# A two-layer graph network with residual and normalisation: the main loop with three row groups in flight on a ring of four PSUM pairs

## The reference

```python
def _sage_conv(x, src, dst, W_l, b_l, W_r):
    agg = jax.ops.segment_sum(x[src], dst, num_segments=N_NODES)
    deg = jax.ops.segment_sum(jnp.ones((src.shape[0],), x.dtype), dst, num_segments=N_NODES)
    return (agg / jnp.maximum(deg, 1.0)[:, None]) @ W_l + b_l + x @ W_r
h = jax.nn.relu(_sage_conv(x, src, dst, W1_l, b1, W1_r))
h = jax.nn.relu(_sage_conv(h, src, dst, W2_l, b2, W2_r))
out = _layernorm(x + h @ W3 + b3, axis=-1)
```

## Time and profile before

| what | value |
| --- | --- |
| median of 3 runs (lowest, highest) | 3318.33 us (3307.94 to 3328.46) |
| span of the profiled execution | 3317.4 us |
| TensorE matmul busy | 2928.3 us (88%) |
| VectorE busy | 2695.7 us (81%) |
| ScalarE busy | 1899.9 us (57%) |
| GpSimd busy | 2689.2 us (81%) |

### The profile page before, as it was taken

One profiled execution on the slowest core, in us unless ns is written; L12 is line 12 of the kernel. 1 busy time (PEld: TensorE's weight loads), 2 busy tenths in 40 slices (PEclk: granted clock), 3 DMA queues, 4 the chain that ended last, 5 costly groups with the idle time before them and its releaser, 6 DMA issues. The chain is left out here.

```text
span 3317.4 us, 57863 instructions
## 1 busy us (share of the span) xinstructions
PE 2928.3 (88%) x18433; PEld 2638.2 (80%) x18433; DVE 2695.7 (81%) x5026; ACT 1899.9 (57%) x3188; POOL 2689.2 (81%) x2614
## 2 busy tenths in 40 slices
PE   6999898999998998999989999999989698787876
PEld 5888887888887888888878888888878687676775
DVE  5778788877888788888988988888888787777775
ACT  4656555556665555655555656556555465555654
POOL 5888888888888888888888888888888767777776
PEclk9999999999999999999999999999999898898988
DMA  3444434434443434434344343444434455555553
GB/s 114 140 145 133 151 128 139 139 127 148 137 139 133 144 130 144 139 127 158 133 142 143 132 157 125 142 142 143 139 127 158 164 199 188 166 201 186 175 191 120
DMA packets 253118, 488.23 MB, mean 147 GB/s; under 512 B 37615, under 2 KB 165206, under 8 KB 253090
## 3 DMA queue, kind: packets, MB, share of 16 engines
q1 hardware_dynamic: 202498, 387.58, 34.2%
q0 software_dynamic: 50176, 99.91, 9.9%
q10 hardware_dynamic: 416, 0.40, 0.0%
HBM read 284.67 MB, written 206.22 MB: 148 GB/s over the span
## 5 line engine op out<-in xcount | busy, mean ns | idle before, releaser
L908 PE MATMUL ps_y<-w_hi,h_hi 128*128 128x256 f32 x1960 | 584.3, 298 | 180.4 <-DVE h_lo L683 180.1
L683 DVE TENSOR_TENSOR h_lo<-h_full,h_hi 128x512 fp32r<-128x512 f32 x784 | 712.3, 946 | 34.3 <-ACT h_hi L511 24.8
L384 POOL TENSOR_SCALAR o<-y,rs,nb 128x256 f32<-128x256 f32 x784 | 659.7, 850 | 1.7 <-DMA out_dram<-o 1.7
L509 ACT ACTIVATE h_full<-ps_h,bias 128x512 f32<-128x512 f32 x784 | 538.3, 687 | 197.1 <-PE ps_h L897 169.5
L908 PE MATMUL ps_y<-w_lo,h_hi 128*128 128x256 f32 x1960 | 572.5, 292 | 0.0
L908 PE MATMUL ps_y<-w_hi,h_lo 128*128 128x256 f32 x1960 | 572.5, 292 | 0.0
L342 POOL DMA_INDIRECT xe<-in_x_dram,e_stage x392 | 412.7, 1053 | 177.2 <-issue 94.8
L908 PEld LDWEIGHTS ps_y<-w_hi,h_hi 128*128 128x128 f32 x1960 | 396.6, 202 | 200.0 <-issue 189.1
L503 ACT CAST xt_hi<-ps_x 128x512 fp32r<-128x512 f32 x392 | 210.9, 590 | 596.1 <-PE ps_x L887 596.1
L669 DVE TENSOR_TENSOR xt_lo<-ps_x,xt_hi 128x512 fp32r<-128x512 f32 x392 | 252.7, 686 | 334.2 <-ACT xt_hi L503 334.0
L396 POOL TENSOR_TENSOR xb<-xn,b_row 128x1024 f32<-128x1024 f32 x196 | 477.1, 2434 | 35.7 <-DVE nb L719 32.2
(11 more groups left out here) (121 smaller groups left out, 7054.1 us busy)
## 6 DMA issues: line engine op xcount, KB each, us to landing
xn<-in_x_dram SPq DMA_DIRECT2D x196, 512.0 KB, 6.6
out_dram<-o SPq DMA_DIRECT2D x196, 512.0 KB
seg<-seg_tab SPq DMA_DIRECT2D x74, 512.0 KB, 4.6
xdb_tab<-xdb SPq DMA_DIRECT2D x49, 512.0 KB, 3.9
h_tab<-src_h SPq DMA_DIRECT2D x49, 512.0 KB
h_tab<-dst_h SPq DMA_DIRECT2D x49, 512.0 KB
xn<-h_tab SPq DMA_DIRECT2D x49, 512.0 KB, 5.2
xb<-xdb_tab SPq DMA_DIRECT2D x49, 512.0 KB, 4.1
```

Of the source, the lines that this page charges most:

```text
L384: ins = nc.gpsimd.tensor_scalar(o[:, b, s], y[:, b, s], rs[:, b, s:s + 1], nb[:, b, s:s + 1], ALU.mult, ALU.add)
L509: nc.scalar.activation(h_full[:, n, k], ps_h[n][:, k], ACT.Relu, bias=bias[:, n, k:k + 1]).then_inc(hf_ok[n], 1)
L683: nc.vector.tensor_tensor(h_lo[:, n, k], h_full[:, n, k], h_hi[:, n, k].bitcast(f32), ALU.subtract).then_inc(hlo_ok[n], 1)
L908: ins = nc.tensor.matmul(ps[:, s // 2, s % 2 * D:(s % 2 + 1) * D], a[:, k, s * P:(s + 1) * P], wx[:, w, k], start=first, stop=end)
```

## The change

Outside the functions printed, the change renames the PSUM pairs, drops `xe_full` and adapts counts. What it does:

- The four pairs become a ring, `pair[0]` to `pair[3]`. At step g (u = g mod 4), `pair[u]` holds the transposes of g+2 and later the second layer of g, `pair[u+1]` the first layer of g+1, `pair[u+2]` the edge quarter, `pair[u+3]` the third layer of g-1.
- TensorE's step becomes: transposes (g+2), first layer (g+1), edge quarter, third layer (g-1), second layer (g).
- Low parts, high parts, the residual and the edge sums `src_h`, `dst_h` are one instruction of 1024 columns each. The relu stays at 512, since its bias differs by half.
- The edge rows are read from PSUM directly, by the cast to `xe_hi`, the subtraction to `xe_lo` and the scans.
- VectorE's step becomes: low part of x (g+2), factors (g-2), low part of the first layer (g+1), edge quarter, residual and moments (g-1), low part of the second layer (g).
- SyncE loads group g+4 as soon as `xb` (g) is made, stores g-2 in step g (before: g-4), and loads `seg` at u = 0 behind that load (before: at u = 1 of the pass ahead of its use, since SyncE's program ran four groups behind).
- The last two groups are normalised before the first `fetch`. Normalisation stays on GpSimd, as four instructions.

```diff
-        xe_full = sb("xe_full", [P, 2, K, G])
...
-        ps_x, ps_h1, ps_h2, ps_y = pb("ps_x"), pb("ps_h1"), pb("ps_h2"), pb("ps_y")
-        ps_h = [ps_h1, ps_h2]
+        pair = [pb(f"pair{n}") for n in range(4)]
...
             def body(i, first, last):
                 for u in range(U):
                     g = i * U + u
-                    if not first:
-                        sp.wait_ge(xt_ps, (g - U + 1) * K)
-                        sp.wait_ge(xb_ok, g - U + 1)
-                        sp.dma_start(xn[:, u], rows(x, g)).then_inc(x_in[u], 16)
-                    if not first:
-                        store(g - U, u % 2)
-                        edge_store(i - 1, u)
-                    if u == 1:
+                    if not last:
+                        sp.wait_ge(xt_ps, (g + 1) * K)
+                        sp.wait_ge(xb_ok, g + 1)
+                        sp.dma_start(xn[:, u], rows(x, g + U)).then_inc(x_in[u], 16)
+                    if u == 0:
                         after(sp, mean_ok, i)
                         sp.dma_start(seg[:, :, :].rearrange("p a g -> p (a g)"),
                                      seg_tab[bass.ds(i, 1), :, :].rearrange("j a g -> j (a g)").to_broadcast([P, 2 * G]))\
                             .then_inc(seg_in, 16)
-            passes(sp, body)
-            store(NG - U, 0)
-            edge_store(NE - 1, 0)
-            edge_store(NE - 1, 2)
+                    if u == 1:
+                        edge_store(i, 0)
+                    if u == 3:
+                        edge_store(i, 2)
+                    if u == 0 and not first:
+                        edge_store(i - 1, 3)
+                    if not (first and u < 2):
+                        store(g - 2, u % 2)
+            body(0, True, False)
+            with sp.Fori(1, NI - 2) as i:
+                body(i, False, False)
+            body(NI - 2, False, False)
+            body(NI - 1, False, True)
             edge_store(NE - 1, 3)
+            store(NG - 2, 0)
...
             load(1, 1)
-            store(NG - 3, 1)
-            sp.wait_ge(y_ok, NG * K)
+            sp.wait_ge(y_ok, NG)
             load_x(0, 0)
-            store(NG - 2, 0)
             sp.wait_ge(y_out[0], 16 * (NG // 2))
             store(NG - 1, 1)
...
+                if last:
+                    for n in (NG - 2, NG - 1):
+                        pool.wait_ge(nb_ok, n + 1)
+                        pool.wait_ge(y_out[n % 2], 16 * (n // 2))
+                        normalise(n, n % 2)
...
-            def normalise_last(g, b):
-                pool.wait_ge(nb_ok, g + 1)
-                pool.wait_ge(y_out[b], 16 * (NG // 2 - 1))
-                normalise(b)
...
             fetch(0, 0)
-            normalise_last(NG - 2, 0)
             fetch(1, 1)
-            normalise_last(NG - 1, 1)
...
-            def evac_x(g, b):
-
-                for k in range(K):
-                    act.wait_ge(xt_ps, g * K + k + 1)
-                    nc.scalar.copy(xt_hi[:, b, k], ps_x[:, k]).then_inc(xhi_ok, 1)
-
-            def evac_h(g, n):
+
+            def high_x(g, b, ps):
+
+                act.wait_ge(xt_ps, (g + 1) * K)
+                nc.scalar.copy(xt_hi[:, b], ps[:, :, :]).then_inc(xhi_ok, 1)
+
+            def high_h(g, n, h, ps):
 
                 for k in range(K):
                     act.wait_ge(l_ps[n], g * K + k + 1)
-                    nc.scalar.activation(h_full[:, n, k], ps_h[n][:, k], ACT.Relu, bias=bias[:, n, k:k + 1]).then_inc(hf_ok[n], 1)
-                    act.wait_ge(hf_ok[n], g * K + k + 1)
-                    nc.scalar.copy(h_hi[:, n, k], h_full[:, n, k]).then_inc(hhi_ok[n], 1)
+                    after(act, hlo_ok[n], g)
+                    nc.scalar.activation(h_full[:, n, k], ps[:, k], ACT.Relu, bias=bias[:, n, k:k + 1]).then_inc(hf_ok[n], 1)
+                act.wait_ge(hf_ok[n], (g + 1) * K)
+                nc.scalar.copy(h_hi[:, h], h_full[:, n]).then_inc(hhi_ok[n], 1)
 
...
-            def edges(i, u):
+            def edges(i, u, ps):
 
                 if u == 0:
-                    for k in range(K):
-                        act.wait_ge(xs_ps, i * K + k + 1)
-                        after(act, run_ok, i * K)
-                        after(act, xs_ok, i)
-                        nc.scalar.copy(xe_full[:, 0, k], ps_x[:, k]).then_inc(xsf_ok, 1)
+                    act.wait_ge(xs_ps, (i + 1) * K)
+                    nc.scalar.copy(xe_hi[:, 0], ps[:, :, :]).then_inc(xshi_ok, 1)
...
-                    evac_h(g, 0)
-                    edges(i, u)
+                    if not (last and u >= 2):
+                        high_x(g + 2, u % 2, pair[u])
                     if not (first and u < 2):
                         deviation(g - 2, u % 2)
-                    if not (last and u == U - 1):
-                        evac_x(g + 1, (u + 1) % 2)
-                    evac_h(g, 1)
-                    edge_parts(i, u)
+                    if not (last and u == 3):
+                        high_h(g + 1, 0, (u + 1) % 2, pair[(u + 1) % 4])
+                    edges(i, u, pair[(u + 2) % 4])
+                    high_h(g, 1, 2, pair[u])
                 if last:
-                    deviation(NG - 2, 0)
-                    deviation(NG - 1, 1)
+                    for n in (NG - 2, NG - 1):
+                        deviation(n, n % 2)
...
+            def low_x(g, b, ps):
+                dve.wait_ge(xhi_ok, g + 1)
+                nc.vector.tensor_tensor(xt_lo[:, b], ps[:, :, :], xt_hi[:, b].bitcast(f32), ALU.subtract).then_inc(xlo_ok, 1)
+
+            def low_h(g, n, h):
+                dve.wait_ge(hhi_ok[n], g + 1)
+                nc.vector.tensor_tensor(h_lo[:, h], h_full[:, n], h_hi[:, h].bitcast(f32), ALU.subtract).then_inc(hlo_ok[n], 1)
+
...
+            def residual(g, b, l3, y_s, ps):
+                dve.wait_ge(l3, (g + 1) * K)
+                nc.vector.tensor_tensor(y[:, b].rearrange("p s d -> p (s d)"), ps[:, :, :].rearrange("p k g -> p (k g)"),
+                                        xb[:, b].rearrange("p s d -> p (s d)"), ALU.add).then_inc(y_s, 1)
...
+            def edges(i, u, ps):
 
                 if u == 0:
+                    dve.wait_ge(xshi_ok, i + 1)
+                    nc.vector.tensor_tensor(xe_lo[:, 0], ps[:, :, :], xe_hi[:, 0].bitcast(f32), ALU.subtract).then_inc(xs_ok, 1)
                     dve.wait_ge(seg_in, 16 * (i + 1))
                     for k in range(K):
-                        dve.wait_ge(xsf_ok, i * K + k + 1)
                         after(dve, run_ok, (i - 1) * K + k + 1)
-                        nc.vector.tensor_tensor_scan(run[:, k], seg[:, 0], xe_full[:, 0, k], run[:, k, G - 1:G], ALU.mult, ALU.add)\
+                        nc.vector.tensor_tensor_scan(run[:, k], seg[:, 0], ps[:, k], run[:, k, G - 1:G], ALU.mult, ALU.add)\
                             .then_inc(run_ok, 1)
...
             def body(i, first, last):
                 for u in range(U):
                     g = i * U + u
-                    if u == 2:
-                        edges(i, u)
-                    low_h(g, 0)
+                    if not (last and u >= 2):
+                        low_x(g + 2, u % 2, pair[u])
                     if not (first and u < 2):
                         factors_rows(g - 2, u % 2)
-                    if u == 3:
-                        edges(i, u)
-                    if not (last and u == U - 1):
-                        low_x(g + 1, (u + 1) % 2)
-                    if u == 2:
-                        edge_parts(i, u)
+                    if not (last and u == 3):
+                        low_h(g + 1, 0, (u + 1) % 2)
+                    edges(i, u, pair[(u + 2) % 4])
                     if first and u == 1:
                         dve.wait_ge(seg_out, 64)
                     if not (first and u == 0):
-                        residual_rows(g - 1, (u + 1) % 2)
-                    if u < 2:
-                        edge_parts(i, u)
+                        residual_rows(g - 1, (u + 1) % 2, pair[(u + 3) % 4])
+                        moments_rows(g - 1, (u + 1) % 2)
+                    low_h(g, 1, 2)
                     if last and u == 2:
 
                         dve.wait_ge(slots_ok, NE)
                         nc.vector.tensor_tensor(h_row[:, :], slots[:, :], base[:, :], ALU.min).then_inc(row_ok, 1)
-                    low_h(g, 1)
-                    if not (first and u == 0):
-                        moments_rows(g - 1, (u + 1) % 2)
                 if last:
                     factors_rows(NG - 2, 0)
-                    residual_rows(NG - 1, 1)
+                    residual_rows(NG - 1, 1, pair[3])
                     moments_rows(NG - 1, 1)
                     factors_rows(NG - 1, 1)
...
-            def ps_x_free(i, u):
+            def edges_left(i, u):
 
                 if u == 0:
-                    pe.wait_ge(xsf_ok, (i + 1) * K)
+                    after(pe, dst_ok, i)
                 if u == 1:
```

(40 more changed lines are left out.)

172 lines of the change are left out of this document (81 added, 91 removed).

## The result

The changed kernel takes 3398.5 us (median of 4, 3393.5 to 3409.9) against 3313.1 for the kernel before: a ratio of 1.0254, 95% interval 1.0218 to 1.0289. It is slower by 2.5%, and outside the range forecast.

The account below looks back on a forecast made before the run. GpSimd was taken to bind the kernel before. A pass of 51.5 us (50.3 + 0.5 + 0.7) instead of 52.74 gave 3317.4 - 60 + 5 = 3262, stated as 3263 us; range 3200 to 3370.

Parts of the forecast that it names:

- its 47.6: TensorE's own work in a main-loop pass, summed from its blocks: 47.6 us, leaving 5 us to spare.
- The new chain through `seg`: Main-loop cycle from GpSimd's `xb` through `seg`, scans, TensorE and `nb` to the next pass's start: 50.3 us.
- The waits it names as signs: Main loop: VectorE's scans wait for `seg` 1 to 5 us a pass, TensorE for scans, GpSimd for `nb` 1 or 2.
- One sign: GpSimd's mean normalising instruction should fall from 0.84 to about 0.73; otherwise GpSimd stays the bound.
- the first rival: GpSimd stays the main loop's bound, longer instructions blocking longer: pass 52.6 us, 3317 us; chance 0.25.
- would upset all of it: Warning that a changed TensorE clock, 0.95 over the run before, would overturn the whole forecast; no size given.
- GpSimd's own pass of 50.5: GpSimd's main-loop pass after the change: 45.3 us undisturbed work, 4.4 disturbance and 0.8 waiting.
- added 0.7: Main-loop allowance, in us a pass, for two nearly equal loops that feed each other missing the larger one's ideal.
- If GpSimd's loss goes with that time, 6.6 becomes 4.4: GpSimd's disturbance in us a pass shrinks with VectorE's time on two SBUF inputs, 18.3 to 12.1 us.
- The sum with squares: GpSimd's loss taken with squared VectorE instruction lengths, 16.6 before and 14.6 after: 6.6 becomes 5.8 us a pass.
- `seg` decides, slower: Rival: `seg` lands in 6.6 us and VectorE loses all three meetings; pass 55.0 us, 3430 us; chance 0.15.
- the +5: Ends of the run, after the main loop: first and third `fetch` shift, adding 5 us (0 to 10).

Follow-up runs that it names:

- e5: Changed kernel with `seg` loaded ahead of the x load and normalisation moved from GpSimd to ScalarE; 3071 us, ratio 0.9234 to the kernel before.
- e2: Changed kernel with TensorE's stall filled by repeating eight transposes four more times; 3405 us, ratio 1.0200 to the kernel before.
- e8: Changed kernel with each `h_lo` made in two instructions of 512 columns; 3394 us, ratio 1.0197 to the kernel before.
- e9: Changed kernel with both TensorE's stall filled by repeated transposes and `h_lo` in halves; 3330 us, ratio 1.0010 to the kernel before.
- e1: Changed kernel with the load of `seg` issued ahead of the wait for `xb` and the x load; 3304 us, ratio 0.9897 to the kernel before.
- e3: Kernel before with `seg` issued only once `xb` of the pass's first group is made; 3334 us, ratio 0.9992 to the kernel before.
- e4: e1 with each `h_lo` made in two instructions of 512 columns; 3205 us, ratio 0.9569 to the kernel before.
- e7: Kernel before with each `h_lo` in one instruction of 1024 columns, once both halves are cast; 3356 us, ratio 1.0102 to the kernel before.
- e11: e5 with each `h_lo` made in two instructions of 512 columns; 3080 us, ratio 0.9246 to the kernel before.

## Why the prediction was wrong

**What held.** GpSimd had no time over before, and TensorE 5 us (e5's 47.48 confirms its 47.6). The new chain through `seg` was named, and its first part was near: `seg` issued 3.2 us after the start of `xb` (3.1 counted), the scans ended after 10.9 (10.1 counted, since the landing took 5.3 and not 4.5). The waits it names as signs appeared on the three engines named, but not as large as it said throughout: VectorE's for `seg` was 3.9 us a pass (1 to 5 said), GpSimd's for `nb` 4.6 (1 to 2 said). One sign misled: a normalising instruction whose mean does not fall from 0.84 to about 0.73 was to speak for the first rival. It fell by busy time to 0.81 (633.5 / 784), and yet `seg` decided.

**The chain was under-sized: 50.3 counted, 54.4 in the pass shown.** Its terms were 10.1 to the scans' end, 36.2 for TensorE and 4.0 from its transposes to `xb`, with 0.5 for the third layer beside them. The pass shown has 11.0 (1509.18 to TensorE's start at 1520.18), 38.5 (to 1558.65) and 5.0 (to 1563.63). The first term was 0.9 short, most of it the landing. The last was 1.0 short: it counted the cast as following the transposes at once, but ScalarE first makes relu and high part of the second layer of 4i+3, and began the cast at 1560.53, 1.9 us after the transposes. The excess of the middle term, 2.3 us, is the clock's. The prediction counted TensorE's blocks at full clock and said that a change of the clock "would upset all of it", but gave TensorE's stall, which it forecast itself ("and TensorE for the scans"), no price. First layer and transposes of `xd` took 6.5 us (1520.18 to 1526.67) in the changed kernel and 4.2 in e2 at a clock of 1.00 (1524.24 to 1528.39). The Trainium skill's page "TensorE: Matmul & The Clock Gate" (Part 1) has the engine at half its clock after idling, and this trace agrees (0.50). The mean of 0.97 in the earlier trace rows hides what one stall costs. e2, with 36.2 us for that term, confirms the price as TensorE's, and shows that paying it back alone is worth nothing.

**The chain through GpSimd was not counted at all.** The prediction set the seg chain (through TensorE) against GpSimd's own pass of 50.5, each by itself, and added 0.7. It did not ask what the late `seg` does to GpSimd's second start. `nb` of 4i-1 is made behind the scans, at 16.4 after the pass began (1525.53 to its release at 1525.77), while GpSimd's work ended 2.7 earlier. Then its three groups follow, and 16.6 + 35.8 (to 1561.58) is 52.4: 2.0 us less than TensorE's chain in the same pass, and already more than the 51.5 forecast. So TensorE's chain set the changed kernel's pass, and GpSimd's took over once TensorE's was shortened (e2). Edit one, 0.1 to 0.2 us; edit both, 1.6 (e2, e8, e9).

**The sum for GpSimd's load came out right by luck.** GpSimd's pass without waits is 54.3 - 4.6 = 49.7, and 50.5 with 0.8 of waits was forecast, the same 49.7. The prediction had the relief come from fewer instructions with two SBUF inputs. But in e1, which has the same few instructions and hardly a wait, the load was back at 52.0. So the term "If GpSimd's loss goes with that time, 6.6 becomes 4.4" fails too: the loss stayed at 6.7 (52.0 - 45.3), and the first rival's 52.6 was the right size for e1. That the relief in the changed kernel came from the waiting, in which the engines cannot meet, is argued, not shown. e3 agrees: there GpSimd waited more before `xb` (59.4 us, 35.7 before) and normalising took less (610.8 us, 659.7 before). e4's 2.0 us says that the length of an instruction counts beyond the time it holds; e7's 0.7 agrees in sign. (The sum with squares belongs to the first rival; the prediction's text points to the second.)

**The rivals.** The second, "`seg` decides, slower", held in its place and its sign: the pass was above 53.3. It had 0.15. Its size (55.0) rested on all three `h_lo` losing and on a landing of 6.6; in truth the landing was 5.3, and the clock's 2.3 us and ScalarE's 1.0 came instead. That its 55.0 lies close to the measured 54.3 is luck. The third fetch came 4.7 us later behind the last `xdb` than before (2719.74 - 2651.0 = 68.7 against 64.1), as the +5 said.

That each of the two conditions is needed is shown: late `seg` without the new order costs nothing (e3), the new order with `seg` earlier costs nothing against the kernel before (e1). Which of the new order's parts is at fault is only argued: the scans ahead of the residual, or TensorE's wait for them. Neither was moved alone. What GpSimd's loss depends on in detail, beyond length, stays open too.

## What to carry to other kernels

When a load is moved behind another engine's step, add up the whole cycle, through each engine that waits for the load and back to that step, and do it for every such path, not only for the longest: here the second was 2 us behind the first, and no single remedy showed a gain. Where TensorE will stall, look in the trace for the granted clock behind a stall of that length, and price the work that follows at it. And where GpSimd binds, look for work that another engine can do: moving 8.7 us of normalising to ScalarE took 4.8 us off the pass (e1 to e5), until TensorE bound. VectorE's instructions with two inputs in SBUF were better short there (e4); where TensorE bound it made no difference (e11).

## What the runs showed of the hardware

- After TensorE stood idle for 4.8 us its granted clock was 0.50 (1.2 GHz) in the stretch of 5.8 us that followed, and its 512-column matmuls began 0.43 us apart instead of 0.23. With repeated transposes in that gap (e2, 1.7 us of idle time left) it stayed at 1.00.
- A four-column GpSimd addition, 0.20 us alone, took 1.18 in the median over 194 times, and never more than 1.27. In the pass shown it stood behind a VectorE subtraction of two SBUF operands that had itself waited for GpSimd's `xb`.
- VectorE instructions with one operand in PSUM were not stretched: the scans were 1257 to 8158 ns with their input in SBUF and 1249 to 1281 with it in PSUM.
- A broadcast load of 512 KB landed in 5.3 us behind an x load, and in 4.5 before.
